# First cross attention: the second of two copies of the shift rows moves from ScalarE to VectorE

## What is computed

```python
qc = _heads(x @ Wcq + bcq)                 # 16 heads of 8
kc = _heads(cross_input @ Wck + bck)       # 1601 keys
vc = _heads(cross_input @ Wcv + bcv)
attc = jnp.einsum('bhqd,bhkd->bhqk', qc, kc) * scale
y = y + jnp.einsum('bhqk,bhkd->bhqd', jax.nn.softmax(attc, axis=-1), vc)
```

## Time and profile before

| | |
|---|---|
| median of 3 runs | 2286.98 us (2262.93 to 2294.28) |
| profiled execution | 2294.59 us, span 2292.4 us, mean granted TensorE clock 0.862 |
| busy share of the span | TensorE 80%, VectorE 51%, ScalarE 42%, GpSimd 23% |
| `stage_long`, 375 to 735 us | TensorE 322.0, VectorE 253.1, ScalarE 261.2, GpSimd 19.2 us busy, clock 0.80 |

### The profile page before, as it was taken

The page is one execution under the profiler, slowest core; times in us unless marked ns, Lnnn a source line. Parts: engine busy times, 40 slices in busy tenths (PEclk is TensorE's granted clock), DMA queues, the critical chain, the costliest instruction groups (busy, mean ns, idle before and its releaser), DMA issues. The chain is left out here.

```text
span 2292.4 us, 42946 instructions
## 1 busy us (share of the span) xinstructions
PE 1837.0 (80%) x16607; PEld 1007.5 (44%) x16607; DVE 1177.9 (51%) x2374; ACT 969.5 (42%) x1576; POOL 524.5 (23%) x392
## 2 busy tenths in 40 slices
PE   2774584999998339989899498579999999997598
PEld 1452361232233316654466265324445445454365
DVE  2664487777773335448642466434555555541322
ACT  1442262777776222211354244214554554553133
POOL 2112312000000000006544000024445445442000
PEclk8896696788887659999999779759999999998699
DMA  8414322211110221000000000021121121100010
GB/s 221 126 52 127 88 67 47 44 43 43 32 29 1 97 56 42 28 14 1 1 1 1 1 2 16 5 54 37 41 51 38 41 51 36 42 23 1 19 37 28
DMA packets 111896, 96.47 MB, mean 42 GB/s; under 512 B 21696, under 2 KB 97128, under 8 KB 111208
## 3 DMA queue, kind: packets, MB, share of 16 engines
q1 hardware_dynamic: 111720, 94.04, 15.7%
HBM read 51.30 MB, written 19.86 MB: 31 GB/s over the span
## 5 line engine op out<-in xcount | busy, mean ns | idle before, releaser
L2102 DVE TENSOR_REDUCE ta_mxp<-ps 128x1 f32<-128x401 f32 x512 | 267.2, 570 | 275.9 <-PE ps L2021 275.8
L1154 DVE TENSOR_REDUCE ac_mxp<-ps 128x2 f32<-128x802 f32 x256 | 244.7, 991 | 91.6 <-PE ps L1070 90.2
L2125 ACT ACTIVATE ta_prob<-ps 128x2048 f32<-128x2048 f32 (+1 forms) x112 | 196.5, 1755 | 146.9 <-PE ps L2057 146.9
L1183 ACT ACTIVATE cT<-ps 128x512 f32<-128x512 f32 (+1 forms) x416 | 225.7, 595 | 62.9 <-PE ps L1095 54.9
L1109 PE MATMUL ps<-cT 128*32 128x256 f32 (+1 forms) x1664 | 157.5, 456 | 0.5 <-ACT cT L1183 0.5
L2021 PE MATMUL ps<-ta_kb,ta_qb 96*128 96x401 bf16 x512 | 138.6, 355 | 16.4 <-DMA ta_kb<-ta_kh 12.2
L2053 PE MATMUL ps<-qxf,ta_k 32*128 32x256 f32 (+1 forms) x1664 | 133.6, 405 | 12.8 <-ACT ta_shiftT L2143 9.2
L2565 PE MATMUL ps<-xT,e_wi 128*128 128x512 f32 x256 | 116.1, 613 | 15.0 <-DMA e_wd<-in_e_down 10.2
L1070 PE MATMUL ps<-ac_kb,ac_qz 50*128 50x401 bf16 x512 | 100.7, 401 | 25.2 <-DMA ac_qb<-qc 18.5
L2575 PEld LDWEIGHTS ps<-e_wd,e_hid 128*128 128x128 f32 x1024 | 116.9, 192 | 7.6 <-issue 7.6
L2188 POOL TENSOR_TENSOR yT<-ta_prob 128x1024 f32<-128x1024 f32 x40 | 94.0, 2350 | 110.1 <-ACT ta_prob L2125 93.6
(11 more groups left out here) (323 smaller groups left out, 3507.0 us busy)
## 6 DMA issues: line engine op xcount, KB each, us to landing
ta_kb<-ta_kh SPq DMA_DIRECT2D x128, 100.1 KB
ac_kb<-kc SPq DMA_DIRECT2D x192, 50.0 KB
ta_kb<-ta_kl SPq DMA_DIRECT2D x64, 100.1 KB
v<-p_vt SPq DMA_DIRECT2D x16, 256.0 KB, 3.2
a_vs<-v SPq DMA_DIRECT2D x32, 128.0 KB, 2.7
e_wi<-in_e_in SPq DMA_DIRECT2D x8, 512.0 KB, 3.5
e_wd<-in_e_down SPq DMA_DIRECT2D x16, 256.0 KB, 3.6
kc<-c_part SPq DMA_DIRECT2D x12, 300.0 KB, 3.0
```

The lines of the kernel that those rows point to most:

```text
L1154: v.tensor_reduce(mxp[:, qt * G + 2 * gg:qt * G + 2 * gg + 2, c:c + 1], k.ps[:, i % 2 * 2:i % 2 * 2 + 2, 0:401], AX.X, ALU.max).then_inc(s ...
L1183: a.activation(prob[0:rows, n % 3, h, :], k.ps[0:rows, bank(("part", n, h)), :], ACT.Exp, scale=scale).then_inc(exp_done.s, 1)
L2102: v.tensor_reduce(mxp[:, qt * G + g, c:c + 1], k.ps[:, turns.bank(slot), 0:401], AX.X, ALU.max).then_inc(scores_read.s, 1)
L2125: a.activation(prob[0:rows, n % 3, :, 0:w], k.ps[0:rows, 2:6, 0:w], ACT.Exp, scale=scale).then_inc(exp_done.s, 1)
```

## The change

One of the two copies, that of the odd heads (PSUM partitions 32 and 33 to rows 96 and 97 of `qb`), is taken from ScalarE and given to VectorE, right behind the instruction that makes the low part of the negated maximum. ScalarE keeps the even heads' copy. VectorE waits for `shift_t` (the products of `shift_rows`) ahead of its copy. TensorE waits for two semaphores, `shift_in` and the new `shift_low`, at tile 0 of a step and where it frees the bank of the shift rows. The new semaphore is the existing one named "masked".

```diff
@@ TensorE, free()
                     elif kind == "shift":
-                        pe.wait_ge(shift_in.s, shift_in.at(2 * n + 2))
+                        pe.wait_ge(shift_in.s, shift_in.at(n + 1))
+                        pe.wait_ge(shift_low.s, shift_low.at(n + 1))
@@ TensorE, transposed_scores()
                     if t == 0:
-                        pe.wait_ge(shift_in.s, shift_in.at(2 * s + 2))
+                        pe.wait_ge(shift_in.s, shift_in.at(s + 1))
+                        pe.wait_ge(shift_low.s, shift_low.at(s + 1))
@@ VectorE, end of a step
                     v.scalar_tensor_tensor(out=low, in0=mx[:, :], scalar=-1.0, in1=high,
                                            op0=ALU.mult, op1=ALU.subtract).then_inc(negmax.s, 1)
+                    v.wait_ge(shift_t.s, shift_t.at(s + 1))
+                    v.tensor_copy(qb[64 + SR:64 + SR + 2, s % NBUF, :, :].rearrange("p g n -> p (g n)"),
+                                  k.ps[32:34, bank(("shift", s, 0)), 0:2 * N]).then_inc(shift_low.s, 1)
@@ ScalarE, shift()
                     a.wait_ge(shift_t.s, shift_t.at(s + 1))
-                    for h in range(2):
-                        a.activation(qb[64 * h + SR:64 * h + SR + 2, s % NBUF, :, :].rearrange("p g n -> p (g n)"),
-                                     k.ps[32 * h:32 * h + 2, bank(("shift", s, 0)), 0:2 * N],
-                                     ACT.Copy).then_inc(shift_in.s, 1)
+                    a.activation(qb[SR:SR + 2, s % NBUF, :, :].rearrange("p g n -> p (g n)"),
+                                 k.ps[0:2, bank(("shift", s, 0)), 0:2 * N], ACT.Copy).then_inc(shift_in.s, 1)
```

More of the change, by code:

```diff
@@ L959, in stage_long @@
     (scores, scores_read, negmax, shift_t, shift_in, st_ready, exp_done, probs_used, out_read, spread_t, logged, inverted,
-     divided, vec, filled, vfilled, widened) = (k.sems[n] for n in (
+     divided, vec, filled, vfilled, widened, shift_low) = (k.sems[n] for n in (
          "scores", "scores_read", "negmax", "shift_t", "shift_in", "st_ready", "exp_done", "probs_used", "out_read", "mm2",
-         "act", "inverted", "divided", "vec", "filled", "vfilled", "pool"))
+         "act", "inverted", "divided", "vec", "filled", "vfilled", "pool", "masked"))
     ops = [k.sems["ops%d" % n] for n in range(NBUF)]
@@ L1208, in _ @@
                         invert(n)
-    for s_, n_ in ((scores, NS * SLOTS), (scores_read, NS * SLOTS), (negmax, NS), (shift_t, NS), (shift_in, 2 * NS),
+    for s_, n_ in ((scores, NS * SLOTS), (scores_read, NS * SLOTS), (negmax, NS), (shift_t, NS), (shift_in, NS), (shift_low, NS),
                    (st_ready, 2 * NS * KT), (exp_done, 2 * NS * KT), (probs_used, NS * KT), (out_read, NS), (spread_t, NS),
```

## The result

Over 20 runs of each, the changed kernel has a median of 2292.5 us (2280.5 to 2304.9) and the kernel before one of 2289.3 us (2256.2 to 2306.7). The ratio reported is 1.0092, with a 95% interval from 1.0059 to 1.0124. It compares only the runs within 1.5% of each kernel's own fastest (2256.2 and 2280.5 us), which leaves out 10 of the 20 runs before, all above 2290 us, and none of the changed kernel's. The two medians are 0.1% apart. What differs between the two sets is the low end: 7 of the 20 runs before are under 2280 us, and none of the changed kernel's.

A forecast was written before the change was run, and what follows sets the result against it. The prediction took TensorE as the bound at low clock and the chain's order, mostly ScalarE behind the shift, at full clock. Gains of 0.2 + 0.35 + 0.37 = 0.9 us, rounded to 1.0, turned 2287.0 into 2286.0 us, range 2258 to 2298.

The forecast's parts named there:

- the chance of 0.96: Whole kernel: time stays within 2% (46 us) of before, with 0.02 given to each side beyond.
- ScalarE's copy, 0.06 us at a full-clock shift: Behind four later full-clock shifts: the next exponential starts 0.06 us earlier, not 0.59, since tile 12's scores come at 607.10.
- The first shift, 0.35 us; the last, 0.37: First shift: 0.35 of 0.51 us stay, VectorE delaying a plain slot; last: tile 0's scores 0.37 us earlier.
- the prediction's 0.9 us: Whole kernel: sum of the gains at full-clock shifts, first shift and last shift, 0.2 + 0.35 + 0.37 us less.
- VectorE's copy at 0.69 us, hidden: Behind each full-clock shift: VectorE's added copy takes 0.69 us and its gaps of 0.21 and 1.31 us absorb it, costing 0.
- The point from which it would decide, 1.2 us: Behind a shift: from 1.2 us of copy, VectorE's first reduction ends after TensorE wants its banks again.
- The added waits at 0: TensorE's two added waits per step, at tile 0 and freeing the shift bank: taken as 0, at most 3.2 us altogether.
- The copies side by side: Behind each shift: both engines read one bank at once; the rival, copies in turn, cost 1.3 us more, chance 0.07.
- the clock re-rolls: Rival, cross attention: a small time shift moves TensorE clock falls into or out of intervals, 2276 or 2296 us, chance 0.20.
- two or three falls: Cross attention: size taken for changed TensorE clock falls, 7 to 12 us either way.
- all intervals alike: Cross attention: all 15 intervals at 18.8 or 23.8 us, 282 or 357 instead of 323, so between 2246 and 2321 us.
- VectorE becomes the chain: Rival, tail of each interval: VectorE's copy delays it, 6.3 to 13.6 us more, middle 10, so 2297 us, chance 0.10.

The follow-up runs named there:

- x5: Kernel before, with tile 10's weighing issued ahead of the shift products instead of behind them; median 2262.6 us, ratio 0.9922.
- x9: Changed kernel, with tile 10's weighing issued ahead of the shift products; median 2249.1 us, ratio 0.9865.
- x12_filler: Kernel before, with 20 small identity products in TensorE's idle ahead of each shift but the first, second set of runs; median 2256.5 us, ratio 0.9879.
- x10_after_filler: Changed kernel, with 20 small identity products in TensorE's idle ahead of the shifts; median 2253.1 us.
- x4: Changed kernel, but VectorE makes both copies and ScalarE none; median 2279.6 us, ratio 1.0011.
- x3: Changed kernel, but ScalarE makes both copies as before, so only the added semaphore and TensorE's added waits remain; median 2294.1 us, ratio 1.006.
- x7: Changed kernel, but ScalarE copies its two rows a second time into an unread tile; median 2295.5 us, ratio 0.9924.
- x6: Kernel before, with 20 small identity products in TensorE's idle ahead of each shift but the first; median 2252.8 us, ratio 0.9891.

## Why the prediction was wrong

The time itself, 2292.5 us, lies in the range (2258 to 2298), and within 2% of before, as the chance of 0.96 had it. That confirms little: the range is as wide as the scatter of the kernel before, and a change of 1 us can't be seen in it. Wrong are the direction (1 us less was forecast, and the ratio reported is 1.0092) and the size of what moved beside the structure.

- *ScalarE's copy, 0.06 us at a full-clock shift.* Right: 18.72 for 18.78 us, and the reason as well, with an addition that x5 and x9 brought. Tile 12's scores and ScalarE's copies were two bounds 0.06 us apart; the prediction named only the one that was left.
- *The first shift, 0.35 us; the last, 0.37.* Measured 0.43 at the first (3.27 to 2.84 us from the shift to tile 1's scores) and 0.46 at the last (2.39 to 1.93 us from the shift to tile 0's scores). The clock fell behind that shift in the one trace and not in the other, but x12_filler and x10_after_filler have it at full clock in both, and give 0.47, so it is the structure's. Summed, the prediction's 0.9 us (which it carried on as 1.0) is 1.1 by the traces.
- *VectorE's copy at 0.69 us, hidden.* Right: 0.686 us on average, gap before the fourth reduction 1.31 to 1.30, idle ahead of the shift unchanged. The point from which it would decide, 1.2 us, fits x4.
- *The added waits at 0.* Right where they are already satisfied, by x3 and x7. At the first shift TensorE stands at them, and there they cost 0.09 us in x3. In the changed kernel tile 0's scores come 0.41 us earlier (1.89 to 1.48), not the 0.51 of the prediction.
- *The copies side by side.* Right: both start in the same moment and take 0.59 and 0.69 us. The Trainium skill, "PSUM — Partial Sum Buffer", section "PSUM bank collisions raise a hardware error", says that different quadrants of a bank can be accessed at the same time; this trace agrees.
- *The clock.* This is the step that failed. A re-roll of the clock was in the prediction as a rival, but it took the spread of the three runs as noise around one time, the same for both kernels, and gave the rival "the clock re-rolls" 0.10 each way, as "two or three falls". The runs of before instead fall into two kinds, 23 of 118 from 2256 to 2270 us and most of the others from 2282 to 2309 us (seven lie between, up to 2275.4), and by the trace of x3 the first kind is a run in which the clock doesn't fall from some interval to the end, 38 us at once. None of the changed kernel's 44 runs is of it. The lowest of the three runs shown, 2262.9 us, was by its time one of them, and its distance to the next, 24 us, was the sign that I read as scatter. The bound of "all intervals alike", 2246 us, was worked out and then treated as an extreme.
- *Two readings of the clock.* That more activity releases it, which the prediction took from the Trainium skill ("TensorE: Matmul & The Clock Gate", "Part 1: The HAM clock gate") and weighed as leaning to the fast side, agrees with x6 (clock 1.00 with the idle filled). But the change did not touch that idle (1.54 us before and after), and moved only the distance between its occurrences.
- *A slip.* The upper end, 2298, is called the middle of the rival "VectorE becomes the chain", which is 2297. It changes nothing.

What the change costs, then: typical runs are not slower (median of its 44 runs 2290.8 us; median of the 66 runs of before beside them that are not low 2294.5 us), but there are no low runs, so its mean is higher (2291.0 against 2286.0 us for 83 runs of before, one run of 2829 us left out). The 0.9% of the ratio compares a set without low runs to the faster part of a set that has them, as the control with the kernel before itself shows.

What stays open: why intervals of 18.77 us can hold the full clock to the end with 1.54 us of idle in each, while none of 18.72 us was seen to. With 18.90 us (x4) the clock held for three intervals in a row, fell, and held again. No run moves the interval between 18.72 and 18.77 us by other means than ScalarE's second instruction, and none tells what starts a low run.

## What to carry to other kernels

When one engine's instruction comes off a chain, look for the bound right behind it: here 0.06 of 0.59 us came off, and the rest only when the weighing of another tile was moved as well. Where TensorE's clock changes within a stage, cut the stage into its periods and count how many run at which clock; a spread in the runs may be two ways of running, and here the choice between them went with a change of 0.3% in the period. A short idle of TensorE that recurs can be worth filling (here some 37 us), best with work that is due anyway (x5 and x9), and comparing two kernels with the clock held up shows the structure alone.

## What the hardware showed unexpectedly

- With an idle of 1.54 us in every 18.78 us TensorE's clock was at 1.2 GHz for a part of two intervals in three, though not in x3's trace from the fifth on. With 0.97 us, x5's trace has falls in the second to fourth intervals and none from the fifth to the fifteenth, x9's has none after the first; the times of all 18 runs (2242 to 2267 us) fit that.
- After idle, TensorE starts later: 0.15 us from the end of VectorE's last instruction to the shift products with 1.54 us of idle (605.78, that is 605.61 and 0.17 for L1164 in the timeline of before, to 605.93), 0.05 us when products ran up to 0.22 us ahead (561.23 and 0.17, so 561.40, to 561.45 in x6). With 0.97 us of idle it is 0.15 us too (x9: 516.81 and 0.17, so 516.98, to 517.13). That is about the 0.09 us by which the filler shortens the interval. The row of before:

```profile
605.61 0.17 DVE L1164 SCALAR_TENSOR_TENSOR ac_negm<-ac_mx,ac_negm 128x8 bf16<-128x8 f32 x1
```

- A wait of TensorE for a second semaphore that comes last costs some 0.09 us more than a wait for one (x3's first shift, 0.14 us behind the copy's end for 0.05), and nothing measurable where that semaphore has already come (x7, 0.05 us).
- VectorE's copy out of PSUM into bf16 takes 0.686 us for two partitions of 512 elements, and the f32 copy of 128 partitions 0.692.
